# Two cross-attention layers, one core: the short TensorE steps of a pair in two groups, one head later

## What is computed

```python
k = rms_norm((kv @ Wk).reshape(bsz, kv_len, 8, 128), k_norm_w)      # kv = context, in the first layer + latents
v = (kv @ Wv).reshape(bsz, kv_len, 8, 128)
scores = einsum("bhgqd,bhkd->bhgqk", qg, k) / sqrt(128)              # + mask in the second layer
out = einsum("bhgqk,bhkd->bhgqd", softmax(scores), v)
return out.reshape(bsz, q_len, 32 * 128) @ Wo
```

## Time and profile before

| | us |
|---|---|
| Median of 3 runs (1540.56 to 1540.72) | 1540.71 |
| The profiled execution, its own time | 1542.61 |
| Its span, first to last instruction | 1540.8 |
| TensorE busy in the span | 1448.2 (94%) |
| VectorE, ScalarE, GpSimd busy | 1043.0, 764.1, 422.8 |
| Mean granted TensorE clock, of full | 0.989 |

### The profile page before, as it was taken

The page is one execution under the profiler, slowest core; times in us unless marked ns, Lnnn a source line. Parts: engine busy times, 40 slices in busy tenths (PEclk is TensorE's granted clock), DMA queues, the critical chain, the costliest instruction groups (busy, mean ns, idle before and its releaser), DMA issues.

```text
span 1540.8 us, 23740 instructions
## 1 busy us (share of the span) xinstructions
PE 1448.2 (94%) x7942; PEld 1191.0 (77%) x7942; DVE 1043.0 (68%) x1829; ACT 764.1 (50%) x1412; POOL 422.8 (27%) x574
## 2 busy tenths in 40 slices
PE   8988999996999999899999899999799999999998
PEld 6856777775888888779767688888688888777887
DVE  6776766776666666777767666666766666777766
ACT  5745555554445444655547344444444444463443
POOL 2555443344222222105126222222322222201000
PEclk9999999998999999999999999999899999999999
DMA  7453344354333433345434333335233333434242
GB/s 274 151 197 138 137 172 148 133 199 147 127 120 111 135 123 110 137 155 201 125 139 184 116 123 117 124 118 189 73 125 124 116 123 117 151 117 145 83 164 96
DMA packets 65516, 215.13 MB, mean 140 GB/s; under 512 B 16976, under 2 KB 21840, under 8 KB 58160
## 3 DMA queue, kind: packets, MB, share of 16 engines
q1 hardware_dynamic: 65424, 213.95, 40.7%
HBM read 180.76 MB, written 33.16 MB: 139 GB/s over the span
## 4 chain that ended last, share of the span: by engine, by line
PE 63%; DVE 16%; issue 9%; ACT 5%; DMA 4%; POOL 3%; SPq 0%; DVEq 0%; ACTq 0%; POOLq 0%
PE g_kbanks L54 9%; PE g_kbanks L56 8%; PE g_kbanks L55 8%; PE g_pobanks L1712 7%; PE g_ktbank L1725 4%; PE g_vbank L54 4%; PE g_vbank L55 4%; PE g_vbank L56 3%; PE g_pobanks L1700 3%; PE g_sbank L1687 2%; DVE c0a_nmax L1978 2%; DVE c1a_kn L2012 2%; PE g_pobanks L54 1%; PE g_sbank L54 1%; DVE c_cT_r L410 1%
## 5 line engine op out<-in xcount | busy, mean ns | idle before, releaser
L54 PE MATMUL g_kbanks<-c_wkv_r,c_cT_r 128*128 128x512 f32 x768 | 322.5, 420 | 16.3 <-ACT c0a_v L1899 5.0
L56 PE MATMUL g_kbanks<-c_wkv_r,c_cT_r 128*128 128x512 f32 x768 | 304.0, 396 | 0.0
L55 PE MATMUL g_kbanks<-c_wkv_r,c_cT_r 128*128 128x512 f32 x768 | 303.1, 395 | 0.0
L54 PEld LDWEIGHTS g_kbanks<-c_wkv_r,c_cT_r 128*128 128x128 f32 x768 | 146.1, 190 | 45.0 <-DVE c_wkv_r L212 5.3
L56 PEld LDWEIGHTS g_kbanks<-c_wkv_r,c_cT_r 128*128 128x128 f32 x768 | 145.4, 189 | 34.3
L55 PEld LDWEIGHTS g_kbanks<-c_wkv_r,c_cT_r 128*128 128x128 f32 x768 | 146.3, 190 | 21.4
L1608 POOL TENSOR_TENSOR c1a_ms<-c1a_ss,c_const 128x4 f32<-128x4 f32 x64 | 13.7, 214 | 372.0 <-DVE c1a_ss L2007 372.0
L54 PE MATMUL g_vbank<-c_wkv_r,c_cT_r 128*128 128x512 f32 x256 | 106.8, 417 | 0.6 <-DVE c0a_v L2061 0.6
L1608 POOL TENSOR_TENSOR c0a_ms<-c0a_ss,c_const 128x4 f32<-128x4 f32 x64 | 13.7, 214 | 335.8 <-DVE c0a_ss L2007 335.7
L1846 ACT ACTIVATE c1a_p<-c1a_sm,c1a_nmax 128x512 f32<-128x512 f32 x64 | 46.3, 723 | 120.0 <-DVE c1a_nmax L1983 120.0
L56 PE MATMUL g_vbank<-c_wkv_r,c_cT_r 128*128 128x512 f32 x256 | 101.0, 395 | 0.0
(11 more groups left out here) (536 smaller groups left out, 3796.6 us busy)
## 6 DMA issues: line engine op xcount, KB each, us to landing
c_cT_r<-ctx_split_dram SPq DMA_DIRECT2D x48, 1024.0 KB, 5.5
c_cT_r<-ctx_split_dram SPq DMA_DIRECT2D x48, 768.0 KB, 4.8
ctx_split_dram<-c_cT_r SPq DMA_DIRECT2D x16, 1792.0 KB, 6.4
c_wkv<-in_l_wo SPq DMA_DIRECT2D x16, 1024.0 KB, 4.9
...
```

The lines of the kernel that those rows point to most:

```text
L54: nc.tensor.matmul(out, a[0], b[1], start=start, stop=False, skip_group_check=reopen)
L55: nc.tensor.matmul(out, a[0], b[0], start=False, stop=False, skip_group_check=reopen)
L56: return nc.tensor.matmul(out, a[1], b[0], start=False, stop=stop, skip_group_check=reopen)
```

## The change

TensorE's short steps are gathered. After p2 come, in a row, the transposes of one head's probabilities, the score of the next head, `kt` of the previous pair's second key tile, and `pv` of the head just turned; after p7 the same four for the next head and the pair's first key tile. A head's score is one head later than before, and the helpers `scored` and `summed_up` say whose turn it is. Probabilities, their turned form and the masked scores have one buffer instead of two.

The copy of the turned probabilities moves from VectorE to ScalarE (`pt_copy`). The 32 latent rows are turned first, into `zbank` or `y_bank` instead of the keys' bank, and all three of their small operations are on VectorE (`tail_heads`). The second key tile is copied out of `x_bank` by ScalarE (`kb_kept`) and then squared and normalised in SBUF, where `square` and `normalise` read PSUM before. Two value parts go through a buffer of their own (`keep`). At the turn the differences T1 and T4 are on VectorE, and the blocks T3 and B22 are made and split one pair later. After the last pair the ends of both layers are laid out anew in the same way, with one head more.

```diff
+    def turned_t1(self, dve):
+        dve.wait_ge(self.loaded[0], 32)
+        dve.wait_ge(self.loaded[2], 32)
+        self.quick_difference(self.low(self.T1), self.raw[:, self.SPARE, 0, :], self.low(self.B11))
+
+    def turned_t2(self, pool):
+        pool.wait_ge(self.loaded[3], 32)
+        pool.wait_ge(self.summed, 5)
+        self.difference(self.low(self.T2), self.raw[:, self.SPARE, 1, :], self.low(self.T1))
+
+    def turned_t4(self, dve):
+        dve.wait_ge(self.loaded[1], 32)
+        dve.wait_ge(self.summed, 6)
+        self.quick_difference(self.low(self.T4), self.low(self.B21), self.low(self.T2))
+
+    def turned_t3(self, pool):
+        pool.wait_ge(self.summed, 7)
+        self.difference(self.low(self.T3), self.raw[:, self.SPARE, 1, :], self.raw[:, self.SPARE, 0, :])
...
+    keep = s.sb("keep", [P, 2, UW])
+    sm = s.sb("sm", [P, CTX]) if mask is not None else None
     gate = s.sb("gate", [P, 1]) if mask is not None else None
     nmax = s.sb("nmax", [P, UNIT_H])
     rsum = s.sb("rsum", [P, UNIT_H])
     rinv = s.sb("rinv", [P, UNIT_H])
-    p = s.sb("p", [P, 2, KEYS])
-    pT = s.sb("pT", [P, 2, CT, P])
-    pTs = s.sb("pT_stack", [STACK, 2, P], F32R) if tail else None
+    p = s.sb("p", [P, KEYS])
+    pT = s.sb("pT", [P, CT, P])
+    pTs = s.sb("pT_stack", [STACK, P], F32R) if tail else None
...
+    def scored(u, par, side, second):
+
+        if second:
+            return UNIT_H * (u - 1) + 2 * side, u - 1, 1 - par, 2 * side
+        if side:
+            return UNIT_H * (u - 1) + 1, u - 1, 1 - par, 1
+        return UNIT_H * (u - 2) + 3, u - 2, par, 3
+
+    def summed_up(u, par, side, second):
+
+        if side:
+            return UNIT_H * (u - 1) + int(second), u - 1, 1 - par, int(second)
+        return UNIT_H * (u - 2) + 2 + int(second), u - 2, par, 2 + int(second)
...
         def quad(hf, b, par, cycle, u, side, m):
+            if is_at(m, PAIRS // 2):
+                pool.wait_ge(products, made(m - 1, "p4"))
+            if not is_at(m, 0):
+                root(2 * m - 1, 1)
+            if is_at(m, PAIRS // 2):
+                kvw.turned_t3(pool)
...
-                pool.wait_ge(products, made(m, "p5"))
-                kvw.turned_sum(pool, 0)
                 pool.wait_ge(products, made(m, "p6"))
-                kvw.turned_sum(pool, 1)
-                pool.wait_ge(products, made(m, "p4"))
-                kvw.turned_sum(pool, 2)
-            root(2 * m + 1, 1)
-            if is_at(m, PAIRS // 2 - 1):
-                pool.wait_ge(products, made(m, "p7"))
-                kvw.turned_sum(pool, 3)
+                kvw.turned_t2(pool)
 
         def finish():
+            root(2 * PAIRS - 1, 1)
...
+        def p_transpose(a, free, value, bank):
+            if not exists(a):
+                return
             pe.wait_ge(p_scaled, a + 1)
+            if tail:
+                pe.wait_ge(free, value)
+                nc.tensor.transpose(bank[0:SEQ, 0:P], p[:, CTX:KEYS], ident[:]).then_inc(tail_turned, 1)
             need(pe, pt_ready, a)
             for t in range(CT):
-                last = nc.tensor.transpose(ptbank[:, t * P:(t + 1) * P],
-                                           p[:, k % 2, t * P:(t + 1) * P], ident[:])
-            if tail:
-                pe.wait_ge(kt_lo, turned)
-                last = nc.tensor.transpose(ktbank[0:SEQ, 0:P], p[:, k % 2, CTX:KEYS], ident[:])
+                last = nc.tensor.transpose(ptbank[:, t * P:(t + 1) * P], p[:, t * P:(t + 1) * P], ident[:])
             last.then_inc(pt_done, 1)
...
+                pe.wait_ge(tail_ready, a + 1)
+                last = nc.tensor.matmul(obank[:, 0:P], vlat[:, apar, k * HD:(k + 1) * HD], pTs[:, :],
+                                        start=False, stop=True)
             last.then_inc(o_done, 1)
...
             product(side, context.A11, kvw.B11, x_bank, True).then_inc(products, 1)
             if is_at(m, 0):
                 border.turn(pe, 0)
-            if lags(u, side):
-                pv(a - 1, 1 - par if side else par, (2 * side - 1) % UNIT_H)
-            need(pe, k_normed, 2 * m)
             wait_weights(kvw.B21)
+            need(pe, kb_kept, m)
             product(side, context.A12, kvw.B21, y_bank, True).then_inc(products, 1)
             if is_at(m, 0):
                 border.turn(pe, 1)
             else:
-                kt(2 * m - 1, 1, a if on else 0)
+                p_transpose(summed_up(u, par, side, False)[0], va_added, m, zbank)
+                score(*scored(u, par, side, False))
+                kt(2 * m - 1, 1)
+                pv(*summed_up(u, par, side, False), loads)
             wait_weights(kvw.T2)
             pe.wait_ge(p1_kept, m + 1)
             product(side, context.S2, kvw.T2, x_bank, False).then_inc(products, 1)
...
             wait_weights(kvw.T1)
             need(pe, va_added, m)
             product(side, context.S1, kvw.T1, zbank, True).then_inc(products, 1)
-            if on:
-                if side == 0:
-                    wait_unit(u, par)
-                score(a, 1 - par, 2 * side)
             wait_weights(kvw.T3)
             pe.wait_ge(u2_kept, m + 1)
             product(side, context.S3, kvw.T3, x_bank, False).then_inc(products, 1)
-            if on:
-                kt(2 * m, 0, a)
-                score(a + 1, 1 - par, 2 * side + 1)
+            p_transpose(summed_up(u, par, side, True)[0], ka_added, m + 1, y_bank)
+            score(*scored(u, par, side, True))
+            kt(2 * m, 0)
+            pv(*summed_up(u, par, side, True), loads)
             wait_weights(kvw.T4)
             pe.wait_ge(u3_kept, m + 1)
             product(side, context.A22, kvw.T4, x_bank, False).then_inc(products, 1)
-            if on:
-                p_transpose(a, 2 * side, 2 * m + 1)
-            else:
-                kt(2 * m, 0, 0)
             wait_weights(kvw.B22)
             pe.wait_ge(vb_added, m + 1)
             product(side, context.S4, kvw.B22, zbank, False).then_inc(products, 1)
-            if on:
-                if tail and side == 0:
-                    pe.wait_ge(vlat_loaded[1 - par], 48 * (cycle + par))
-                pv(a, 1 - par, 2 * side)
-                p_transpose(a + 1, 2 * side + 1, 2 * m + 1)
...
+        def pt_copy(a):
+            if not exists(a):
                 return
             act.wait_ge(pt_done, a + 1)
-            need(act, o_done, a - 1)
-            for row in range(2):
-                nc.scalar.activation(pTs[row * ROWS:(row + 1) * ROWS, k % 2, :],
-                                     ktbank[0:SEQ, 0:P], ACT.Copy).then_inc(pt_tail, 1)
+            need(act, o_done, a)
+            nc.scalar.activation(pT[:, :, :], ptbank[:, :].rearrange("p (t n) -> p t n", t=CT),
...
+                pt_copy(summed_up(u, par, side, False)[0])
             act.wait_ge(ka_added, m + 1)
             square(2 * m, kn[:, 0, :])
+            if not is_at(m, 0):
+                place_k(2 * m - 1, 3 - 2 * side, par if side else 1 - par, u if side else u - 1)
+                exponential(x1, k1)
             act.wait_ge(products, made(m, "p6"))
-            need(act, o_done, UNIT_H * (u - 1))
-            nc.scalar.activation(v[:, par, 2 * side, :], x_bank, ACT.Copy).then_inc(u2_kept, 1)
+            need(act, va_added, m)
+            nc.scalar.activation(keep[:, 0, :], x_bank, ACT.Copy).then_inc(u2_kept, 1)
+            divide(x1, k1)
             if prepared(hf, m + 1):
                 for i in range(2):
                     context.make_hi(act, *following(hf, b, side), i)
             if last:
-                for i in range(2):
-                    out.make_hi(act, i)
-            if on:
-                exponential(a, 2 * side)
-            act.wait_ge(products, made(m, "p7"))
-            nc.scalar.activation(v[:, par, 2 * side + 1, :], x_bank, ACT.Copy).then_inc(u3_kept, 1)
-            if on:
-                divide(a, 2 * side)
-            place_k(2 * m, 2 * side, par, u)
-            if is_at(m, PAIRS // 2 - 1):
-                for n in range(3):
-                    kvw.turned_hi(act, n)
-            if last:
                 act.wait_ge(products, made(m, "p1"))
                 for i in range(2):
                     wo.make_hi(act, i)
-            if on:
-                exponential(a + 1, 2 * side + 1)
-                tail_heads(a, 2 * side)
+            if turning:
+                kvw.turned_hi(act, 0)
+            if turned:
+                kvw.turned_hi(act, 5)
+                kvw.turned_hi(act, 6)
+            pt_copy(summed_up(u, par, side, True)[0])
+            act.wait_ge(products, made(m, "p7"))
+            need(act, vb_added, m)
+            nc.scalar.activation(keep[:, 1, :], x_bank, ACT.Copy).then_inc(u3_kept, 1)
+            place_k(2 * m, 2 * side, par, u)
+            exponential(x2, k2)
+            if turning:
+                kvw.turned_hi(act, 1)
+            if last:
+                for i in range(2):
+                    out.make_hi(act, i)
```

(23 more changed lines are left out.)

273 lines of the change are left out of this document (130 added, 143 removed).

## The result

The changed kernel takes 1523.85 us (median of 4 runs, 1521.05 to 1524.36) against 1540.72 (1540.56 to 1542.45) in the same comparison: a ratio of 0.9884, 95% interval 0.9867 to 0.9901. That is 17 us faster, where 64 were forecast.

The account below looks back on a forecast made before the run. TensorE was taken to bound the kernel, with waits visible in its starts. Pairs 51.1, turns 10 and starts 4 made 65 us off 1542.6; adjusted to the median, with about 1 us left for hand-overs, 1477, range 1465 to 1492.

Parts of the forecast that it names:

- The pair without waits: Attention loop: if TensorE waits for nothing, pairs take 15.14 us in the first layer, 14.50 in the second; 51.1 us saved.
- The waits in the pair: In each group, ScalarE's copy of turned probabilities ends before `pv` needs it, with cover of 0.25 and 0.18 us.
- the tile's chain: Second key tile, from copy-out to normalised keys: 4.7 us against 5.5 of TensorE's other work, cover 0.8 us.
- the argument that the copy had to leave VectorE: In the pairs, VectorE's 0.69 us copy was late, queued behind context splits; off that engine, the wait goes.
- The turns: One pair between the halves of each layer: splits and differences moved, waits of 6.1 and some 2 us left; 10 us saved.
- rival B: The turns give nothing, as VectorE's splits slow beside GpSimd: 1487 us, its chance included in the forecast range's 0.74.
- The starts: Starts of both layers: p2's waits of 2.2 and 2.9 us for normalised keys go for a 0.60 us copy; 4 us saved.
- The ends: Ends of both layers, with one head more: TensorE's sum unchanged, between 3 us lost and 4 won, taken as 0.
- A: Copy of turned probabilities not covered: about 120 groups wait some 0.3 us each, 1513 us; chance 0.12 in full form.
- C: Slower than before: TensorE waits at `kt` of the second key tile in every pair, 1570 us at 7 us of chain; chance 0.04.

Follow-up runs that it names:

- cover_pt: The changed kernel with one more ScalarE copy out of PSUM, into a scrap buffer, ahead of each copy of the turned probabilities: 1555.80 us, ratio 1.0090.

## Why the prediction was wrong, point by point

- **The pair without waits** (15.14 and 14.50 us): 15.28 and 14.56, with equal halves in the first layer, as the text asked for. The step holds; 0.14 and 0.06 us a pair were missing, in the first layer by some 0.08 us a group that the transposes of keys take ahead of `pv` over the 0.35 of the forecast. Over the 54 full pairs of the table the forecast's gains make 48.7 us, and 44.1 came.
- **The waits in the pair**: the copy ends 0.40 and 0.34 us ahead of `pv`; less the 0.06 of hand-over that the forecast took off, the cover is 0.34 and 0.28 for 0.25 and 0.18. That of the tile's chain is 1.2 for 0.8. Both right in kind, and cover_pt shows what the first would have cost. Among the pairs, the argument that the copy had to leave VectorE was right only for every second one of those with context splits.
- **The turns** (10 us): 3.3. The two waits that it named were 4.29 us (put at 6.1) and 2.12 (put at 2). But the sum had no term for the load of the new weights, on which `pv` waits 3.98 us in the first layer, nor for the half clock around such waits. The first layer's turn got 2.0 us longer and the second's 5.3 shorter. So rival B, that the turns give nothing, came nearer than the forecast, for another reason.
- **The starts** (4 us): 7.8, that is 2.2 up to the first transposes of keys and 5.6 in the first two pairs of each loop; the third pairs, which the forecast counted as full ones, gave 3.6. p2's waits of the earlier trace rows are gone, and the first pairs, which have no head to serve, gain besides. The last step of each loop gained 4.0 and 3.2 us, for which the sum had nothing.
- **The ends** ("between 3 us lost and 4 won, I take 0"): 42 us lost. This is the step that failed, and it is nearly the whole of what the two spans miss, 43.5 us. Pairs, turns and starts were put at 65 and gave 59; the last steps, which the sum left out, gave 7 and hid that. I had counted what work the ends hold, which is nearly unchanged, and not in which order three engines meet there. The bound of 3 us had no row behind it. The rows of the end before would have shown it. In the first layer TensorE waited 1.0 us there for L471 already, at product 10; in the second the same split ended 0.15 us ahead of that product (1384.23 and 1384.38), so no view of waits shows it, but there was no slack either. The diff takes one product earlier against these splits, and a product is 2.8 us. Product 10 then waits 3.95 us in both layers, and product 11, whose split stands behind the copy that TensorE's late transposes hold, 4.12. And between the last head and the normalised input's transposes stood five products before (60 matmuls from 674.10 to 688.25 us) and three now.

Product 10 before, in the first layer, and in the second with VectorE's split ahead of it:

```profile
674.10 0.47 PE L54 MATMUL g_kbanks<-c_wkv_r,c_cT_r 128*128 128x512 f32 x1 [0.97 <-DVE c_wkv_r L471]
```

```profile
1381.88 2.35 DVE L471 TENSOR_TENSOR c_wkv_r<-c_wkv,c_wkv_r 128x1024 fp32r<-128x1024 f32 x2
```

```profile
1384.38 0.47 PE L54 MATMUL g_kbanks<-c_wkv_r,c_cT_r 128*128 128x512 f32 x1
```

None of the rivals was this. The slower ones (A, C) were looked for in the loop, where an error counts 120 times; what came was an error of 21 us that counts twice.
